# Expert rows of a fused graph-and-mixture kernel: first choices scattered in the step that finds their places, second choices around the RMS factors

## What is computed

```python
# layer 1, on layernorm(x)
agg = epsilon * x + einsum('bnm,bmd->bnd', adjacency, x)
h = einsum('bnd,dh->bnh', agg, W1) + b1
h = silu(h * rsqrt(mean(h**2) + 1e-6) * rms_weight)
x = x + einsum('bnh,hd->bnd', h, W2) + b2
# layer 2, on layernorm(x): mixture of 8 experts, 2 per token
gate_scores = einsum('bsd,ed->bse', x, Wg) + bg
topk_scores, topk_idx = top_k(gate_scores, 2)
combine = softmax(topk_scores) spread over the chosen experts
for e in range(8):
    h = relu(einsum('bsd,hd->bsh', x, W1[e]) + b1[e])
    out = out + combine[..., e:e+1] * (einsum('bsh,dh->bsd', h, W2[e]) + b2[e])
x = x + out
```

## Time and profile before

| | us |
|---|---|
| median of 3 runs | 653.26 |
| lowest, highest | 652.2, 655.01 |
| the profiled execution, its own time | 647.74 |
| its span, first to last instruction | 646.0 |
| PE busy | 562.3 (87%) |
| POOL busy | 408.7 (63%) |
| DVE busy | 352.0 (54%) |
| ACT busy | 294.7 (46%) |
| mean granted clock of PE | 0.949 |

### The profile page before, as it was taken

How to read it: one execution, slowest core, us unless ns; L and a number is a source line. 1 busy time by engine, 2 the same in 40 slices (tenths; PEclk the granted TensorE clock), 3 DMA queues, 4 the chain that set the end, 5 groups by cost and what they waited for, 6 DMA issues and landing times.

```text
span 646.0 us, 13035 instructions
## 1 busy us (share of the span) xinstructions
PE 562.3 (87%) x3704; PEld 463.3 (72%) x3704; DVE 352.0 (54%) x1174; ACT 294.7 (46%) x779; POOL 408.7 (63%) x664
## 2 busy tenths in 40 slices
PE   1999878978798789888985899999999999999882
PEld 0467655655466457555764889999999999999850
DVE  2566665765765757554636474445444444544454
ACT  3354544536345445363342345544554554455411
POOL 5244596477664864775566588776667667667750
PEclk9999879999998799889786899999999999999998
DMA  8995414432344134324010567766767666766698
GB/s 364 334 417 214 151 34 150 152 127 92 122 156 150 35 146 151 104 90 148 17 34 21 205 213 265 254 246 253 256 237 258 258 239 237 265 247 242 217 408 365
DMA packets 40519, 127.18 MB, mean 197 GB/s; under 512 B 7776, under 2 KB 19809, under 8 KB 38273
## 3 DMA queue, kind: packets, MB, share of 16 engines
q1 hardware_dynamic: 31232, 108.88, 45.8%
q0 software_dynamic: 8640, 16.93, 7.9%
q10 hardware_dynamic: 576, 0.53, 0.3%
HBM read 61.19 MB, written 24.02 MB: 132 GB/s over the span
## 4 chain that ended last, share of the span: by engine, by line
PE 57%; POOL 17%; issue 8%; DVE 7%; DMA 5%; ACT 4%; SPq 2%; POOLq 0%; ACTq 0%; DVEq 0%
POOL slots L884 10%; PE ps_y L529 9%; PE ps_y L651 8%; PE ps_g L651 8%; PE ps_agg L545 7%; PE ps_t L495 3%; PE ps_h L495 3%; POOL rms_rstd L851 2%; PE ps_agg L638 2%; PE ps_agg L637 2%; PE ps_h L637 2%; PE ps_h L641 2%; PE ps_agg L641 2%; PE ps_h L638 2%; PE ps_t L626 2%
## 5 line engine op out<-in xcount | busy, mean ns | idle before, releaser
L951 POOL DMA_INDIRECT parts<-adj_in x142 | 138.6, 976 | 68.8 <-ACT adj_in L796 52.4
L545 PE MATMUL ps_agg<-adj_in,xn_both 128*128 128x512 f32 x256 | 137.5, 638 | 13.0 <-ACT xn_both L691 13.0
L884 POOL DMA_INDIRECT slots<-rows,dest x128 | 132.0, 1032 | 23.4 <-issue 23.4
L796 ACT ACTIVATE adj_in<-adj_in,share 128x128 f32<-128x128 f32 x142 | 49.4, 395 | 117.3 <-issue 104.4
L700 ACT ACTIVATE hn<-hb 128x512 f32<-128x512 f32 x64 | 40.0, 625 | 83.4 <-DVE hb L1003 83.4
L651 PE MATMUL ps_y<-W2e,hb 128*128 x576 | 70.2, 275 | 0.8 <-issue 0.8
L1215 DVE TENSOR_TENSOR xe_split<-ps_t,xe_split 128x256 fp32r<-128x256 f32 x71 | 30.1, 425 | 73.5 <-ACT xe_split L778 71.3
L651 PE MATMUL ps_g<-W2e,hn 128*128 x560 | 68.1, 275 | 0.0
L651 PEld LDWEIGHTS ps_y<-W2e,hb 128*128 128x128 f32 x576 | 67.3, 192 | 1.0 <-issue 1.0
L545 PEld LDWEIGHTS ps_agg<-adj_in,xn_both 128*128 128x128 f32 x256 | 46.5, 207 | 29.5 <-issue 26.9
L651 PEld LDWEIGHTS ps_g<-W2e,hn 128*128 128x128 f32 x560 | 65.4, 191 | 0.0
(11 more groups left out here) (179 smaller groups left out, 1242.0 us busy)
## 6 DMA issues: line engine op xcount, KB each, us to landing
wcur<-expert_w SPq DMA_DIRECT2D x71, 578.0 KB
adj_in<-in_adjT SPq DMA_DIRECT2D x16, 2048.0 KB, 8.4
adj_in<-slots SPq DMA_DIRECT2D x71, 130.0 KB
expert_w<-parts SPq DMA_DIRECT2D x8, 512.0 KB, 9.4
out<-x_all SPq DMA_DIRECT2D x8, 512.0 KB, 7.0
x_all<-in_x SPq DMA_DIRECT2D x1, 3072.0 KB, 23.8
parts<-adj_in POOLq DMA_INDIRECT x142
expert_w<-in_F1T SPq DMA_DIRECT2D x1, 2048.0 KB, 19.4
```

The lines of the kernel that those rows point to most:

```text
L545: ins = pe.matmul(ps_agg[par][:, :], xn[b % 2][:, m, :], adj_in[par][:, m, :], start=(m == 0), stop=(m == TPB - 1))
L796: ins = act.activation(ye[ku][:, j, :], yb[ku % 2][:, j, :], ACT.Copy, scale=share[ku][:, j:j + 1])
L884: pool.indirect_dma_start(out=slots, out_offset=bass.IndirectOffsetOnAxis(ap=dest[q % 2][:, c, j:j + 1], axis=0), in_=rows[q % 2][:, c, j, ...
L951: pool.indirect_dma_start(out=parts, out_offset=bass.IndirectOffsetOnAxis(ap=goes[u % 8][:, j, :], axis=0), in_=ye[ku][:, j, :], in_offset ...
```

## The change

Five edits, all in the order of work of the first part; no arithmetic changes.

1. POOL: the scatters of group q's first choices move from step q+3 to the end of step q+2, the step in which `places(q)` runs, behind a wait for `s_dest`. The scatters of second choices stay in step q+3, two of them before `rms_factors` and two after it, instead of four first choices before and four second choices after. In even steps the eight `b2` adds go with the eight scatters as before (the second choices, now the earlier ones, take the first four). The tail follows the same pattern, and takes `ln2_factors` of group 14 ahead of `rms_factors` of group 15.
2. PE: `rank(g-2)` moves from between M(6) and M(7) to the middle of `second_layer(g-1)`, between its second and third chunk.
3. DVE: `places(g-2)` moves behind the low part of the aggregate (L1121).
4. DVE: `low_weights` moves from the end of steps 4 to 11 to the place before that, in steps 5 to 12.
5. ACT: in odd steps the first half of `normalise` moves from behind `scale_hidden` to the head of the step.

```diff
@@ tensor, step @@
                 M(6)
-                if has(g, 2):
-                    rank(g - 2)
                 M(7)
                 if has(g, 1):
                     if g == 1:
                         pe.wait_ge(s_const, 16)
-                    second_layer(g - 1, range(HC))
+                    second_layer(g - 1, (0, 1))
+                if has(g, 2):
+                    rank(g - 2)
+                if has(g, 1):
+                    second_layer(g - 1, (2, 3))
@@ scalar, step @@
             def step(g, par, b):
+                if par == 1 and has(g, -1):
+                    normalise(b + 1, 0)
                 if has(g, 1):
                     for j in range(GT):
                         sum_squares(g - 1, j)
...
                     scale_hidden(g - 1)
-                if par == 1 and has(g, -1):
-                    normalise(b + 1, 0)
@@ gpsimd @@
-            def scatter_rows(q, c, b=None):
+            def scatter_rows(q, c, tiles, b=None):
 
-                for j in range(GT):
+                for j in tiles:
...
-                        rest_by_b2(b, c * GT + j)
+                        rest_by_b2(b, (1 - c) * GT + j)
...
+                own_b2 = b if par == 0 and has(g, 3) else None
                 if has(g, 3):
-                    pool.wait_ge(s_dest, g - 2)
                     pool.wait_ge(s_row2, g - 2)
-                    scatter_rows(g - 3, 0, b if par == 0 else None)
+                    scatter_rows(g - 3, 1, (0, 1), own_b2)
                 if has(g, 1):
                     rms_factors(g - 1)
                 if has(g, 3):
-                    scatter_rows(g - 3, 1, b if par == 0 else None)
+                    scatter_rows(g - 3, 1, (2, 3), own_b2)
                 if par == 0 and has(g, -2):
                     pool.wait_ge(s_mv1, b + 2)
                     ln1_factors()
+                if has(g, 2):
+                    pool.wait_ge(s_dest, g - 1)
+                    scatter_rows(g - 2, 0, range(GT), own_b2)
                 order.end()
             first_part(pool, step, NG - 1)
 
             q = NG - 1
             order.step((NG + 1) * 6)
+            ln2_factors(q - 1)
+            pool.wait_ge(s_row2, q - 1)
+            scatter_rows(q - 2, 1, (0, 1))
             rms_factors(q)
-            ln2_factors(q - 1)
-            pool.wait_ge(s_dest, q - 1)
-            pool.wait_ge(s_row2, q - 1)
-            scatter_rows(q - 2, 0)
-            scatter_rows(q - 2, 1)
+            scatter_rows(q - 2, 1, (2, 3))
+            pool.wait_ge(s_dest, q)
+            scatter_rows(q - 1, 0, range(GT))
             ln2_factors(q)
-            pool.wait_ge(s_dest, q)
             pool.wait_ge(s_row2, q)
-            for c in range(2):
-                scatter_rows(q - 1, c)
+            scatter_rows(q - 1, 1, range(GT))
@@ vector, step @@
-                if has(g, 2):
-                    places(g - 2)
+                if 5 <= g < 5 + E:
+                    low_weights(g - 5)
                 dve.wait_ge(s_aggh, g + 1)
                 dve.tensor_tensor(aggT_lo[:, :], ps_agg[par][:, :], aggT_hi[:, :].bitcast(FP32),
                                   ALU.subtract).then_inc(s_agg, 1)
+                if has(g, 2):
+                    places(g - 2)
                 if has(g, 1):
                     add_second_layer(g - 1)
-                if 4 <= g < 4 + E:
-                    low_weights(g - 4)
```

More of the change, by code:

```diff
@@ L942, in _ @@
             for c in range(2):
-                scatter_rows(q, c)
+                scatter_rows(q, c, range(GT))
             def scatter_results(t, k):
```

## The result

The changed kernel takes 634.74 us (median of 4 runs, 633.93 to 639.66) against 652.73 for the kernel before on the same chip (4 runs, 651.22 to 655.01): a ratio of 0.9742, with an interval of 0.9691 to 0.9793 (the two medians alone give 0.9724), or -18.0 us. The prediction was 644.7, its range 636 to 658.

What follows compares the result with a forecast made beforehand. The group-step loop through POOL, with PE's wait for hidden rows and the half clock behind it, was taken as the bound. Steps -7.1, tail -1.9 and step 1 +0.4 gave -8.6: 644.7 us, range 636 to 658.

Steps and rivals of the forecast that it cites:

- The loop over POOL: Group steps: places, scatters and factors summed to 16.87 us from second layer to first hidden transpose, against 16.47 before.
- If the hidden rows come 2 us earlier, my loop over POOL is wrong: Sign for the profile after: hidden rows 2 us earlier would refute the POOL sum and mean a larger gain.
- I take four steps in ten at the cold price: Group steps: 0.4 of 1.56 us half-clock cost added to 20.63, giving 21.25 a step, -7.1 over 13 steps.
- well below that: PE's even-step gaps of 1.8 and 1.9 us were called well below the waits that cold steps followed.
- passes about 2.5: Slower rival: clock stays low through hidden transposes if PE's normed-row wait passes about 2.5 us; 659 us, chance 0.20.
- no gap reaches 3: Argument for the case of all steps at full clock: none of PE's gaps would reach 3 us.
- all warm: Rival: every group step at full clock, 20.63 us throughout, 636.5 us in all; chance 0.14.
- The same difference from the median: Whole kernel: profiled 647.74 lay 5.5 below the runs' median; the -8.6 was applied to 653.26, giving 644.7.
- The tail: After step 15: second layer 2.0 us sooner, last factors delayed 1.1, tile 7 on time (-0.8); together -1.9.
- at 0: ACT, odd steps: normalise's four instructions, under 2 us, fit into its idle 5.11 us and cost nothing.
- Step 1's +0.4: ACT in step 1: normalise's factors come just when the squares begin and push them, estimated at +0.4 us.
- delays the places by 2.7, which is in the sum: Rank inside the second layer delays the places by 2.7 us, counted in the POOL loop and not priced separately.

Runs made afterwards that it cites:

- e16: The changed kernel with the tail's last layer-norm factors moved ahead of group 14's first-choice scatters: 629.38 us, ratio 0.9657.
- e8: The changed kernel run again unaltered, for its spread and a second profile: 633.63 us, ratio 0.9696.
- e5: The changed kernel with PE kept busy by idle-time transposes before its wait for the normed rows: 633.84 us, ratio 0.9701.
- e3: The kernel before with only the rank inside the second layer and the places behind the low part: 652.62 us, ratio 0.9995.
- e7: The changed kernel without the early low weights and the early normalise half (edits 4 and 5): 643.08 us, ratio 0.9825.
- e13: e7 with PE kept busy by the same transposes as in e5: 638.22 us, ratio 0.981.
- e11: The changed kernel with only the normalise half put back behind the scaling of the hidden rows: 638.84 us, ratio 0.9802.
- e6: The changed kernel with both rank and places put back where they were before: 610.41 us, ratio 0.9353.
- e10: The changed kernel with the rank alone put back between M(6) and M(7): 633.43 us, ratio 0.9692.
- e1: The kernel before with PE running 20 idle-time transposes while it waits for the hidden rows: 632.1 us, ratio 0.9672.
- e17: e2 with add_eps behind the places and the tail's last layer-norm factors ahead of group 14's first-choice scatters: 594.8 us, ratio 0.9128.
- e2: The kernel before with POOL's new scatter order and its tail alone, the other edits left out: 607.62 us, ratio 0.9298.

## Why the prediction was off, step by step

**The loop over POOL was right in its size.** Predicted: scatters 3.53 after the second layer; measured 3.68 and 3.87. The prediction had the places wait for the rank alone, with DVE free. That holds in even steps, where the rank ends at +2.05. In odd ones they stand behind the low part, which waits for ACT and ends at +2.38, and they end at +3.06 instead of 2.67. POOL's waking: 0.86, measured 0.81 between the end of the places and the scatter. Normed rows: waits of 2.6 and 1.8, measured 2.67 and 1.69. RMS factors at 14.2, measured 14.28; in the mean of the thirteen steps they stand at 14.02 in e16, as the sum has it (16.87 - 2.85), and at 13.57 before. The waits for the hidden rows were to be 1.4 into odd and 1.9 into even steps; at the full clock (e16) they are 0.94 and 1.40. Two readings of the prediction were off without weight: the normed rows into an even step come by its own terms at 11.4, not 11.6 (3.53 + 5.42 + 1.32 + 1.11), and before PE waited 0.8 for them in four even steps, not 0.1. The hidden rows are no earlier than before, as I said, and a step at the full clock was to take 20.63; it takes 20.37 (e16), because the way from the RMS factors to the second layer is 0.26 shorter. I said "If the hidden rows come 2 us earlier, my loop over POOL is wrong"; they don't.

**The step that failed is the clock's: "I take four steps in ten at the cold price".** At that price (1.56) the right number is none in ten; the profiled execution has two in thirteen, at 2.1 and 3.3. I had seen that the odd steps' first gap was in the range behind which the clock falls, and that what runs cold there has slack, and then charged it 1.56 all the same. In e8 cold stretches do follow odd steps' waits, and cost 0.09 a step instead of the 0.62 of the sum (20.46 against 20.37 in e16). Over thirteen steps, the measured 20.46 against the predicted 21.25 is 10.3 us: 6.9 of them are this step, 3.4 the shorter step at the full clock. e5 shows it from the other side. The waits' length, from which I had argued in three places ("well below that", "passes about 2.5", "no gap reaches 3"), is no guide: behind 3.00 (e8) the clock fell and behind 2.98 (e16) it didn't, in the same step, and behind step 3's 1.95 it fell in the profiled execution, at a cost of 2.1, and stayed at 1.00 in e8. The case I called "all warm", 636.5, is the one nearest to what came, in its price though not in the clock, and it had a chance of 0.14.

**Before was dearer than its profile.** "The same difference from the median" was a second mistake. Before's profiled execution was cold in eleven steps of thirteen and took 21.80 a step. A typical one takes 22.06 (e3, cold in twelve, with a stretch of some 7 us in five of them instead of three), and the change removes that too: 0.26 x 13 = 3.4 us that the sum could not see. The profiled execution's own clock, 0.949, would have told me only if I had held it against the other runs' 0.932 to 0.943. The Trainium skill ("TensorE: Matmul & The Clock Gate", section on what is actually happening) has the clock judged in a rhythm that doesn't start with the kernel, so that one kernel can come out differently each time. The spread of e7, 639.2 to 649.4 for the same order of work, agrees with it. I cited that rule and said it changed no term; it should have told me that a count of cold steps from one profile is a sample.

**The tail had the wrong sign: -1.9 predicted, +3.0 measured** (38.50 against 35.53, e8 against e3). I had the last factors delayed by 1.1 behind four scatters. They stand 8.94 after the second layer in e8 (347.34 - 338.40), 5.95 after it before. The four scatters take 7.18 and not 5.42, since a gap of 2.10 lies behind the first of them. PE then waits 4.52 for its rows (1.51 before), and the clock falls on what follows. So they come 3.0 later instead of 1.1. The gain I booked ahead of the tail's second layer, 2.0, came to 1.35 (20.82 in e8 against e3's 22.17), while the way behind it grew by 4.3 (17.68 against 13.36). Tile 7 was to be on time; it still waits 0.49 in e8 and 0.85 in the profiled execution.

**Edit 5 was not free.** I put its four instructions into ACT's idle 5.11 "at 0". That was right where they are put, and missed what their absence from the old place does: with late places the odd step hangs on ACT's high part, and edit 5 frees it by 0.55, worth some 4 us of the change (e13 against e5, which differ by edit 4 as well). Step 1's +0.4 didn't show: its second layers start at 51.62 in e8 and 51.59 in e3. Edit 4 at 0 fits the traces in this loop: in even steps the low part ends at +2.05 with it and at +1.52 without it (e16, e13), and the places, which wait for the rank, end at +2.87 in both. No pair of runs takes it alone at the full clock; e7 and e11, which differ by it alone, take 643.08 and 638.84, with more half clock in e7. In the shorter loop it costs 3.8.

**The sum, made anew**, e3's span to e8's: steps 13 x (20.46 - 22.06) = -20.8; tail +3.0; start and experts -0.5; in all -18.3, and 650.7 - 632.4 is 18.3.

**What I never priced was edit 3 by itself.** The prediction has "delays the places by 2.7, which is in the sum". It is the largest term but POOL's order: without it (e6 against e10) the kernel is 23.0 us faster. It stood inside a loop that I compared only with before, so that it showed as "no earlier than before". Taken apart, POOL's order gives -45.7, the late places take 23.0 back and edits 4 and 5 some 3.

Open: whether e1's transposes on top of e17 would give more, and what the floor of the loop is then. Open too is what decides whether the clock falls in a wait, since the same step order gave both. Four tenths of e17's chain between 200 and 240 are scatters and `b2` adds of POOL (29.2% and 11.7%), and PE's waits in e17 are short:

```profile
PE ps_y L502 <- DVE rows L1032: 9.7, 10, 2.7
PE ps_h L495 <- ACT hn L705: 6.7, 8, 0.9
```

## What to carry to other kernels

Price each edit of a bundle against the others, not only the bundle against before: one that delays the input of a queue which another has just made critical can take back half of the gain (23.0 of 45.7 us here). Keep an idle PE busy before you reorder anything (e1), since it prices the clock in one run and tells how much of the reordering is worth having. And hold the profiled execution's time and clock against those of the other runs before its cold steps are counted.

## What the runs showed of the hardware

Transposes of a 128x128 identity keep the clock up: 20 of them in a gap of some 3 us took the mean clock of the kernel from 0.932 to 0.947 up to 0.981 to 0.983, and 21 us off its time (e1). They are no guarantee: one step of e5 ran cold in spite of them. The Trainium skill ("TensorE: Matmul & The Clock Gate", part on PE-mode transpose) says that the full clock does not engage for transposes in PE's transpose mode, because they don't count as busy in the same way. These runs don't bear that out, and the measurement decides; the trace shows them as MATMUL and doesn't say which mode they ran in.

A half-clock stretch has a price of its place and its length. In e8, behind idles of 2.59 to 3.00, it was over before the hidden rows and cost about 0.2; behind one of 2.99 in e7 it went on for 11 us and cost 3.3. In e16 the clock stayed at 1.00 behind five of the six same idles, of 2.66 to 2.98. So neither the fall nor the length of the stretch can be read from the idle before it.

A scatter woken by DVE starts 0.81 after the end of the work it waits for (in the change and in e2), close to the 0.86 behind ACT. In the tail, the second scatter of one run of scatters waits longer than the usual 0.17 and nothing in the trace says for what: 1.57 before, 2.10 in e8, 1.52 in e16. I didn't find the cause.
